# Attention scores per head on eight places of the TensorE array, with scores and transposed probabilities in four shared PSUM banks

## The chip, the cores and the metric

One Trainium2 chip, one core of it. The metric is the device time of one execution in microseconds; the kernel before took 2920.33 us as the median of three runs (2918.25 to 2920.56). TensorE is called PE here, VectorE DVE, ScalarE ACT, GpSimd POOL, and SyncE (which issues the transfers) SP.

## The reference

128 graphs of 64 nodes with 384 features, in float32, go through four layers, each followed by a residual and a layer norm:

```python
x = _layernorm(x + L0(x, adj))   # attention, 12 heads of 32; bias adj + adj
x = _layernorm(x + L1(x, adj))   # attention masked by adj > 0, bias beta * adj
x = _layernorm(x + L2(x, adj))   # directed graph convolution, two inner layers
x = _layernorm(x + L3(x, adj))   # attention like L0; bias adj
```

L0 and L3 compute, per graph and head, `softmax(q k^T * scale + bias) v`, then an output product with Wo and a bias bo; L1 has biases bq and bk, masks with `adj > 0` and has no output product. The weights are 384 x 384.

## The kernel before

The program runs five passes over all 8192 rows one after the other: an attention pass for L0, one for L1, two passes for L2, and an attention pass for L3. Only the attention passes (`attention_pass`, L143) are touched. Every pass reads its rows from memory and writes them back.

**Tiling.** A *unit* is 128 rows, that is two graphs; a *group* is four units (512 rows); a pass has 16 groups, 64 units. The first two and the last two groups are written out, the others run in a loop of pairs (`over_groups`, L49). The place of a unit within its group is called s, 0 to 3.

**The stages of a unit n on the engines.** Queries and keys are projected for a whole group (512 columns, L413) with the features on the partitions, values per unit (L407). Each projection is nine matmuls: three feature tiles and three products of high and low parts. ACT evicts the query (L555, L557) and the key. Of the key it makes two copies (L561, L564): one has the odd heads of each 64 features zeroed, the other the even ones, by the factor `even_odd`. The scores (L434) are twelve matmuls a unit: for each of three feature tiles, both graphs and both halves of 64 partitions, one product of 64 rows by 128 columns gives two heads. In the trace each shows as two records of 128 columns, 24 a unit. They go to `ps_s` (two banks). DVE scales them and adds the bias (L686), takes the maximum (L693) and in L0 and L3 the minimum (L695). POOL subtracts the maximum (L342), ACT takes the exponential (L607), DVE sums it (L700) and inverts the sum, POOL multiplies (L351, only in L0 and L3). PE transposes the probabilities, six transposes of 128 x 128 a unit (L447) into `ps_t` (two other banks), ACT evicts them (L602), and PE multiplies them with the values (L470 in L0 and L3, L466 in L1) into `ps_o`. In L0 and L3 ACT and DVE split the result into a high part (L617) and a low part (L733), PE multiplies with Wo (L485), and DVE adds the residual (L742), takes its statistics (L746, L749) and normalizes (L758). In L1 DVE scales the result (L729), POOL adds the residual (L331), and DVE takes the statistics.

**The order of the work is written out by hand.** Each engine executes its list in order and waits on semaphores. On PE a unit of the loop is:

```python
scores(n, par, s)
fill(i, par, s, 0)
probs_T(n - 1, ps % 2)
fill(i, par, s, 1)
values(n - 1, ppar, ps)
if wo: fill(i, par, s, 2)
scores_may(...)
if not wo: fill(i, par, s, 2)
output(n - 1, ps % 2)
```

`fill` issues the projections and the row transposes of the next groups. The table `BETWEEN` (L229) says which: between scores and transposes there is nothing at s=0 and s=1, and one projection at s=2 (a key) and s=3 (a value). On DVE a unit is: the residual and statistics of n-2, L686 and the maximum and minimum of n, the normalization of n-2, the low part of n-1, the sum of n, and the low parts of the next rows (`fill`). In L0 and L3 the residual of n-2 waits for the output product that PE issues at the end of its unit n-1.

**Waits around the change.** `probs_T` on PE (L439) waits for the probabilities (POOL, or ACT in L1) and for ACT to have evicted the halves of `ps_t`. `scores_may` (L417) waits until DVE has read the scores of the unit before.

**Start and passes.** `Shared` (L62) issues the four weights of L0 with one transfer each (`load`, L117) while DVE zeroes the value buffers (L115); the block ends when all engines are through. Each pass begins with its first rows (L250), two transfers of the value bias (L254), other small transfers, and the first edges (L263). The weights of the next pass are loaded during a pass, by the same `load`.

Of the kernel before, what the change touches and what calls it, by code (L numbers as in the profile page):

```python
# [21 lines left out]
P = 128  # L22
# [10 lines left out]
HEAD_STEP = 84  # L33
MASKED = -9000000000000000.0

SPLIT = ((0, 0), (1, 0), (0, 1))

# [24 lines left out]
class Shared:  # L62


    def __init__(self, nc, ctx, first_mats):
# [12 lines left out]
        self.even_odd = sb("even_odd", [P, 2])  # L78
# [6 lines left out]
        c_heads = nc.alloc_semaphore("c_heads")  # L85

        with nc.Block() as block:
# [5 lines left out]
            def _(pool):  # L93
# [8 lines left out]
                nc.gpsimd.memset(self.even_odd[:, :], 0.0).then_inc(c_heads, 1)  # L102
                pool.wait_ge(c_heads, 1)
                for head in range(4):
                    nc.gpsimd.memset(self.even_odd[32 * head:32 * head + 32, head % 2:head % 2 + 1], 1.0).then_inc(c_heads, 1)
# [37 lines left out]
def attention_pass(nc, tag, src, dst, adj, weights, scale, transposed, wo, bv, bo, beta, edge_factor, groups,  # L143
# [16 lines left out]
    with ExitStack() as ctx:  # L160
# [18 lines left out]
        k2 = [a.sb(f"k2{b}", [P, KT, 2, ROWS]) for b in range(2)]  # L179
        v2, even_odd = shared.v2, shared.even_odd  # L180
        qkb = a.sb("qkb", [P, 2, KT])
        kbm = a.sb("kbm", [P, 2, KT])
# [22 lines left out]
        c_zero = a.sem("c_zero")  # L205
        pe_w, act_w, dve_w = a.sem("pe_w"), a.sem("act_w"), a.sem("dve_w")
# [7 lines left out]
        dve_x, dve_off, dve_bias, dve_kb, dve_sc, dve_mx, dve_mn, dve_sum, dve_inv, dve_o = (  # L214
            a.sem(x) for x in ("dve_x", "dve_off", "dve_bias", "dve_kb", "dve_sc", "dve_mx", "dve_mn",
# [6 lines left out]
        n_small = 2 + (bo is not None) + (2 if row_bias_cols else 0) + (beta is not None)  # L222
# [140 lines left out]
        def _(pe):  # L363
# [1063 lines left out]
```

## Time and profile before

| what | value |
|---|---|
| median of three runs | 2920.33 us |
| the profiled execution | 2920.63 us |
| its span | 2918.9 us |
| mean granted PE clock | 0.963 of full |
| PE busy | 2676.6 us, 92% |
| DVE busy | 2204.6 us, 76% |
| POOL busy | 1906.2 us, 65% |
| ACT busy | 1441.8 us, 49% |

The span runs from the first to the last instruction of the profiled execution; the time of that execution also has what lies around it. The busy times are unions of an engine's instructions. The attention passes lie at about 9 to 655 us (L0), 661 to 1204 us (L1) and 2267 us to the end (L3); the two passes of L2 stand between. The loading of weights into the array (PEld) is shown apart from the matmuls (PE); both belong to one engine.

### The profile page before, as it was taken

How to read it: one execution, taken by the hardware profiler on the slowest of the kernel's cores; microseconds unless marked ns; L12 is line 12 of the kernel's file. 1: busy time of each engine (PE TensorE's matmuls, PEld its weight loads, DVE VectorE, ACT ScalarE, POOL GpSimd, SP SyncE). 2: the span in 40 equal slices, each digit the busy share in tenths (PEclk: the TensorE clock that was granted, in tenths of full speed). 3: DMA queues.
4: the chain of work that ended last, by engine and by line, in shares of the span. 5: the costliest groups of instructions: out<-in, count | busy, mean ns of one | idle time of the engine just before them, and what ended most of it. 6: DMA issues, size and time to landing. Idle time of an engine off the chain costs nothing. (4 is left out here: it accounts for less than half of the span.)

```text
span 2918.9 us, 67000 instructions
## 1 busy us (share of the span) xinstructions
PE 2676.6 (92%) x22942; PEld 2351.3 (81%) x22942; DVE 2204.6 (76%) x3795; ACT 1441.8 (49%) x2968; POOL 1906.2 (65%) x2229
## 2 busy tenths in 40 slices
PE   7999999977999999599999888888887899999996
PEld 6888888866778778599999877777776688888885
DVE  4888888874777777577777667777777488888886
ACT  4555555535566666344444344444444455555553
POOL 2766766762666666577777567767776267766766
PEclk9999999988999999699999989999999999999998
DMA  3222222113222222312212132222221122222211
GB/s 108 70 67 68 66 66 68 55 42 96 78 76 81 81 76 63 99 53 68 64 55 67 56 102 71 69 68 71 69 68 48 57 70 67 68 66 68 66 58 39
DMA packets 179134, 200.54 MB, mean 69 GB/s; under 512 B 56516, under 2 KB 179016, under 8 KB 179016
## 3 DMA queue, kind: packets, MB, share of 16 engines
q1 hardware_dynamic: 179016, 198.99, 22.2%
q8 instruction: 71, 1.16, 0.2%
q14 instruction: 47, 0.39, 0.0%
HBM read 136.03 MB, written 62.91 MB: 68 GB/s over the span
## 5 line engine op out<-in xcount | busy, mean ns | idle before, releaser
L413 PE MATMUL l_ps_p<-l_xT,l_w 128*128 128x512 f32 x2592 | 677.5, 406 | 6.5 <-DVE l_xT L655 4.5
L1088 PE MATMUL l_ps_h<-l_w,l_hT 128*128 128x384 f32 x3456 | 678.9, 342 | 0.0
L1088 PEld LDWEIGHTS l_ps_h<-l_w,l_hT 128*128 128x128 f32 x3456 | 612.6, 191 | 2.6
L413 PEld LDWEIGHTS l_ps_p<-l_xT,l_w 128*128 128x128 f32 x2592 | 467.8, 189 | 110.7 <-issue 8.3
L342 POOL TENSOR_TENSOR l_pr<-l_sc,l_st 128x768 f32<-128x768 f32 x192 | 289.4, 1507 | 368.7 <-DVE l_st L693 341.1
L1178 ACT ACTIVATE l_hp<-l_hf 128x384 fp32r<-128x384 f32 x256 | 134.7, 526 | 474.5 <-DVE l_hf L1300 470.4
L312 POOL TENSOR_TENSOR v<-v,l_bvs 128x768 f32<-128x768 f32 x192 | 368.6, 1920 | 0.0
L999 POOL TENSOR_TENSOR l_hp<-l_hf,l_hp 128x384 fp32r<-128x384 f32 x256 | 272.0, 1062 | 134.4 <-ACT l_hp L1178 131.7
L407 PE MATMUL l_ps_p<-l_w,l_xT 128*128 128x384 f32 x1728 | 349.5, 347 | 7.6 <-ACT l_k L561 3.7
L574 ACT ACTIVATE v<-l_ps_p 64x192 f32<-64x192 f32 x768 | 250.5, 326 | 188.0 <-PE l_ps_p L407 179.1
L407 PEld LDWEIGHTS l_ps_p<-l_w,l_xT 128*128 128x128 f32 x1728 | 291.6, 188 | 27.3 <-issue 8.8
L602 ACT ACTIVATE l_pT<-l_ps_t 128x512 f32<-128x512 f32 (+1 forms) x384 | 167.7, 491 | 182.9 <-PE l_ps_t L447 180.4
L485 PE MATMUL l_ps_y<-l_w,l_oT 128*128 128x384 f32 x1152 | 236.0, 351 | 23.8 <-DVE l_oT L733 20.5
L485 PEld LDWEIGHTS l_ps_y<-l_w,l_oT 128*128 128x128 f32 x1152 | 214.7, 196 | 30.0 <-issue 18.5
L351 POOL TENSOR_TENSOR l_pr<-l_pr,l_st 128x768 f32<-128x768 f32 x128 | 188.7, 1474 | 74.2 <-DVE l_st L711 68.1
L700 DVE TENSOR_REDUCE l_st<-l_pr 128x12 f32<-128x768 f32 x192 | 182.0, 948 | 37.8 <-ACT l_pr L607 37.7
L686 DVE SCALAR_TENSOR_TENSOR l_sc<-l_ps_s,l_sbias 128x768 f32<-128x768 f32 x192 | 183.9, 958 | 30.1 <-PE l_ps_s L434 24.1
L1300 DVE TENSOR_TENSOR l_hf<-l_ps_h,l_sides 128x384 f32<-128x384 f32 x256 | 142.3, 556 | 68.1 <-PE l_ps_h L1088 62.1
L564 ACT ACTIVATE l_k<-l_ps_p,even_odd 128x512 f32<-128x512 f32 x192 | 121.8, 685 | 138.1 <-PE l_ps_p L413 138.1
L693 DVE TENSOR_REDUCE l_st<-l_sc 128x12 f32<-128x768 f32 x192 | 183.0, 953 | 6.7
L607 ACT ACTIVATE l_pr<-l_pr 128x768 f32<-128x768 f32 x192 | 163.0, 849 | 44.5 <-POOL l_pr L342 42.3
L1104 PE MATMUL l_ps_c<-l_hp,l_aT 128*128 128x384 f32 x768 | 162.0, 345 | 23.7 <-POOL l_hp L999 22.9
(129 smaller groups left out, 4761.1 us busy)
## 6 DMA issues: line engine op xcount, KB each, us to landing
rows<-l_yo SPq DMA_DIRECT2D x256, 192.0 KB, 1.9
l_xa<-rows SPq DMA_DIRECT2D x64, 768.0 KB, 5.0
l_xr<-rows SPq DMA_DIRECT2D x192, 192.0 KB, 2.4
l_xa<-in_x SPq DMA_DIRECT2D x16, 768.0 KB, 4.8
l_xr<-in_x SPq DMA_DIRECT2D x64, 192.0 KB, 2.4
out<-l_yo SPq DMA_DIRECT2D x64, 192.0 KB, 1.9
l_edge<-in_adj SPq DMA_DIRECT2D x80, 128.0 KB, 2.3
raw<-in_L_gnn_Wq SPq DMA_DIRECT2D x3, 576.0 KB, 5.8
```

The costliest lines, as they stand in the source:

```text
L312: nc.gpsimd.tensor_tensor(got, got, bvs[:, :, :].unsqueeze(1).to_broadcast([P, GPU, PAIRS, 64]), ALU.add).then_inc(pool_v, 1)
L342: nc.gpsimd.tensor_tensor(pr[b][:, :, :], sc[b][:, :, :], st[b][:, 0, :].unsqueeze(2).to_broadcast([P, HEADS, NODES]), ALU.subtract).then_ ...
L351: nc.gpsimd.tensor_tensor(pr[b][:, :, :], pr[b][:, :, :], st[b][:, 5, :].unsqueeze(2).to_broadcast([P, HEADS, NODES]), ALU.mult).then_inc( ...
L407: last = nc.tensor.matmul(bank[:, :D], rows[:, l, t, o * P:(o + 1) * P], W[2][:, r, t, :], start=c + t == 0, stop=c == 2 and t == KT - 1)
L413: last = nc.tensor.matmul(bank[:, :], W[m][:, l, t, o * P:(o + 1) * P], rows[:, r, t, :], start=c + t == 0, stop=c == 2 and t == KT - 1)
L485: last = nc.tensor.matmul(ps_y[:, :D], oT[b][:, l, t, :], W[3][:, r, t, :], start=c + t == 0, stop=c == 2 and t == KT - 1)
L574: i = nc.scalar.activation(v2[gpar][64 * odd:64 * odd + 64, GPU * u + g2, :, 32 * odd:32 * odd + 32], got[:, :, odd, :], ACT.Copy)
L686: nc.vector.scalar_tensor_tensor(out=sc[b][:, :, :], in0=logits[:, :, :NODES], scalar=scale, in1=sbias[par][:, s, :].unsqueeze(1).to_broad ...
L693: nc.vector.tensor_reduce(st[b][:, 0, :], sc[b][:, :, :], AX.X, ALU.max).then_inc(dve_mx, 1)
L700: nc.vector.tensor_reduce(st[b][:, 2, :], pr[b][:, :, :], AX.X, ALU.add).then_inc(dve_sum, 1)
L999: nc.gpsimd.tensor_tensor(hp[b][:, m, 1, :], hf[b][:, m, :], hp[b][:, m, 0, :].bitcast(F32), ALU.subtract).then_inc(pool_h, 1)
L1088: last = nc.tensor.matmul(ps_h[m][:, :D], hT[gpar][:, l, t, s * P:(s + 1) * P], W[m][:, r, t, :], start=c + t == 0, stop=m != SELF and c = ...
```

## The change

Each head's scores become a matmul of their own: contraction over 32 partitions, 64 query columns loaded, 64 key columns moved. Four heads by two graphs stand on eight places of the array (`tile_position`), and the key needs one copy without zeroed heads. The heads are kept in the order of *slots*: slot 3m + t holds head 4t + m (`head_of` gives it), so that the four heads of a feature tile lie in four different banks. `ps_s` has four banks; each slot has 170 places, the first 64 for the scores, the next 64 for transposed probabilities, and `ps_t` is gone. The transposes become twelve a unit: per graph and pair of slots, 64 partitions by 128 columns. ACT evicts them per graph. Since scores and transposes share banks, PE waits before the transposes of n until DVE has read the scores of n + 1, and before the scores until ACT has evicted the transposes. The weights Wv and Wo, and the value bias, are loaded in the slots' order: by 12 transfers each (rows or columns by slot) in place of one or two. The factor `even_odd`, the two bias copies made with it, and their waits are gone.

```diff
-HEAD_STEP = 84
+HEAD_STEP = 170
+NATURAL, ROWS_BY_SLOT, COLUMNS_BY_SLOT = range(3)
+def head_of(slot):
+    return 4 * (slot % KT) + slot // KT
...
     def load(self, sp, mats, free=None):
-        for m, mat in enumerate(mats):
+        for m, (mat, order) in enumerate(mats):
             if free:
                 free(m)
-            sp.dma_start(self.raw[m][:, :, :], mat.rearrange("(t p) n -> p t n", p=P)).then_inc(self.s_raw[m], 16)
-            self.loads[m] += 1
+            if order == ROWS_BY_SLOT:
+                for slot in range(HEADS):
+                    t, b = divmod(slot, 4)
+                    head = head_of(slot)
+                    sp.dma_start(self.raw[m][32 * b:32 * b + 32, t, :], mat[32 * head:32 * head + 32, :]).then_inc(self.s_raw[m], 16)
+                self.loads[m] += HEADS
+            elif order == COLUMNS_BY_SLOT:
+                for t in range(KT):
+                    for q in range(4):
+                        natural = mat[t * P:(t + 1) * P, :].rearrange("p (k m d) -> p m k d", m=4, k=KT)[:, q, :, :]
+                        sp.dma_start(self.raw[m][:, t, 96 * q:96 * q + 96].rearrange("p (k d) -> p k d", k=KT),
+                                     natural).then_inc(self.s_raw[m], 16)
+                self.loads[m] += 4 * KT
+            else:
+                sp.dma_start(self.raw[m][:, :, :], mat.rearrange("(t p) n -> p t n", p=P)).then_inc(self.s_raw[m], 16)
+                self.loads[m] += 1
...
-        ps_s = a.ps("ps_s", [P, 2 * 512])
-        logits = ps_s[:, 8:8 + HEADS * HEAD_STEP].rearrange("p (h x) -> p h x", x=HEAD_STEP)
-        ps_t = a.ps("ps_t", [P, 2 * 512])
+        ps_s = a.ps("ps_s", [P, 4 * 512])
+        by_head = ps_s[:, 8:8 + HEADS * HEAD_STEP].rearrange("p (h x) -> p h x", x=HEAD_STEP)
+        logits, turned = by_head[:, :, :NODES], by_head[:, :, NODES:2 * NODES]
...
-            for odd in range(2):
-                heads = bv.rearrange("(a h o d) -> a h o d", a=1, o=2, d=32)[:, :, odd, :]
-                sp.dma_start(bvs[64 * odd:64 * odd + 64, :, 32 * odd:32 * odd + 32],
-                             heads.to_broadcast([64, PAIRS, 32])).then_inc(s_small, 16)
+            for slot in range(HEADS):
+                h, odd = divmod(slot, 2)
+                head = bv.rearrange("(a d) -> a d", a=1)[:, 32 * head_of(slot):32 * head_of(slot) + 32]
+                sp.dma_start(bvs[64 * odd:64 * odd + 64, h, 32 * odd:32 * odd + 32],
+                             head.to_broadcast([64, 32])).then_inc(s_small, 16)
...
                 if counted(n):
                     pe.wait_ge(dve_sc, n)
+                if counted(2 * (n - 1)):
+                    pe.wait_ge(act_pT, 2 * (n - 1))
...
             def scores(n, par, s):
                 for t in range(KT):
                     for g in range(GPU):
-                        for r in range(2):
-                            c, q = s * P + g * NODES, slice(64 * r, 64 * r + 64)
-                            h = PAIRS * r + 2 * t
-                            last = nc.tensor.matmul(logits[g * NODES:(g + 1) * NODES, h:h + 2, :NODES],
-                                                    qT[par][q, t, c:c + NODES], k2[par][q, t, :, c:c + NODES],
-                                                    start=True, stop=True)
+                        for m in range(4):
+                            c, q = s * P + g * NODES, slice(32 * m, 32 * m + 32)
+                            last = nc.tensor.matmul(logits[g * NODES:(g + 1) * NODES, KT * m + t, :],
+                                                    qT[par][q, t, c:c + NODES], kT[par][q, t, c:c + NODES],
+                                                    start=True, stop=True, tile_position=(32 * m, g * NODES))
...
                 pe.wait_ge(pool_p if wo else act_e, n + 1)
+                pe.wait_ge(dve_sc, n + (2 if inside(n + 1, units) else 1))
+                pe.sem_inc(pe_waited, 1)
                 for h in range(PAIRS):
-                    if h in (0, 4):
-                        if counted(2 * n - 1 + (h == 4)):
-                            pe.wait_ge(act_pT, 2 * n - 1 + (h == 4))
-                    last = nc.tensor.transpose(ps_t[:, h * P:(h + 1) * P], pr[b][:, 2 * h:2 * h + 2, :], ident[:, :])
-                    if h in (3, 5):
-                        last.then_inc(pe_t, 1)
+                    for g in range(GPU):
+                        q = slice(g * NODES, (g + 1) * NODES)
+                        last = nc.tensor.transpose(turned[:, PAIRS * g + h, :], pr[b][q, 2 * h:2 * h + 2, :], ident[q, q])
+                        if h == PAIRS - 1:
+                            last.then_inc(pe_t, 1)
...
-                        for j in range(2):
-                            if row_bias_cols:
-                                i = nc.scalar.activation(k2[gpar][:, o, j, :], bank[:, :], ACT.Identity,
-                                                         bias=kbm[:, j, o:o + 1], scale=even_odd[:, j:j + 1])
-                            else:
-                                i = nc.scalar.activation(k2[gpar][:, o, j, :], bank[:, :], ACT.Copy,
-                                                         scale=even_odd[:, j:j + 1])
+                        if row_bias_cols:
+                            i = nc.scalar.activation(kT[gpar][:, o, :], bank[:, :], ACT.Identity, bias=qkb[:, 1, o:o + 1])
+                        else:
+                            i = nc.scalar.activation(kT[gpar][:, o, :], bank[:, :], ACT.Copy)
...
-                for half, (lo, hi) in enumerate(((0, 4), (4, 6))):
-                    act.wait_ge(pe_t, 2 * n + half + 1)
+                for g in range(GPU):
+                    act.wait_ge(pe_t, 2 * n + g + 1)
...
-                    nc.scalar.activation(pT[b][:, lo:hi, :], ps_t[:, lo * P:hi * P].rearrange("p (h q) -> p h q", q=P),
+                    nc.scalar.activation(pT[b][:, :, g * NODES:(g + 1) * NODES], turned[:, PAIRS * g:PAIRS * (g + 1), :],
```

Wq and Wk are loaded in one transfer as before; Wv of L0 and L3 by rows, Wv of L1 and Wo of L0 and L3 by columns. The passes of L2 are not changed.

## Rows read from the trace of the kernel before

**Rows 1.** The page's part 1: engine, busy us (share of the span) xinstructions.

```profile
PE 2676.6 (92%) x22942; PEld 2351.3 (81%) x22942; DVE 2204.6 (76%) x3795; ACT 1441.8 (49%) x2968; POOL 1906.2 (65%) x2229
```

**Rows 2.** Busy time by stretch, layer 3: window, length, busy (count) per engine, PEclk, DMA share.

```profile
2303.00:2867.00 564.00, 559.55 (x5259) 472.56 (x5251) 479.09 (x768) 306.12 (x658) 392.23 (x355) 1.00 0.21 62
```

**Rows 3.** Groups by line and form, PE: busy us, mean ns | idle before, releasers.

```profile
L434 PE MATMUL l_ps_s<-l_k,l_qT 64*64 64x128 f32 x4608 | 174.3, 282 | 0.8 <-DVE l_sc L686 0.8
...
L447 PE MATMUL l_ps_t<-ident,l_pr 128*128 128x128 f32 x1152 | 166.2, 281 | 12.8 <-ACT l_pr L607 9.5 <-POOL l_pr L351 3.2
...
L470 PE MATMUL l_ps_o<-l_pT,v 128*64 128x64 f32 x3072 | 123.7, 228 | 11.1 <-ACT l_pT L602 9.2
```

**Rows 4.** Timeline of layer 3, a unit at s=0: start us, us, engine, line.

```profile
2527.95 0.64 PEld L434 LDWEIGHTS l_ps_s<-l_k,l_qT 64*64 64x64 f32 x24 [0.24 <-issue]
...
2528.05 0.56 DVE L742 TENSOR_TENSOR l_res<-l_ps_y,l_xr 128x384 f32<-128x384 f32 x1 [0.92 <-PE l_ps_y L485]
...
2528.83 0.64 PEld L447 LDWEIGHTS l_ps_t<-ident,l_pr 128*128 128x128 f32 x6 [0.24 <-issue]
...
2529.58 0.96 DVE L686 SCALAR_TENSOR_TENSOR l_sc<-l_ps_s,l_sbias 128x768 f32<-128x768 f32 x1
```

**Rows 5.** Timeline of layer 3, units at s=2 and s=3.

```profile
2509.64 0.96 DVE L686 SCALAR_TENSOR_TENSOR l_sc<-l_ps_s,l_sbias 128x768 f32<-128x768 f32 x1
...
2510.86 0.81 PEld L447 LDWEIGHTS l_ps_t<-ident,l_pr 128*128 128x128 f32 x6
...
2519.53 1.53 PEld L407 LDWEIGHTS l_ps_p<-l_w,l_xT 128*128 128x128 f32 x9 [0.17 <-issue]
...
2520.29 0.96 DVE L686 SCALAR_TENSOR_TENSOR l_sc<-l_ps_s,l_sbias 128x768 f32<-128x768 f32 x1
...
2521.05 0.75 PEld L447 LDWEIGHTS l_ps_t<-ident,l_pr 128*128 128x128 f32 x6
...
2523.71 0.83 PEld L470 LDWEIGHTS l_ps_o<-l_pT,v 128*64 128x64 f32 x24 [0.42 <-ACT l_pT L602]
...
2526.27 1.75 PE L485 MATMUL l_ps_y<-l_w,l_oT 128*128 128x384 f32 x9
```

**Rows 6.** Timeline of layer 1, units at s=0 and s=1.

```profile
917.58 0.64 PEld L447 LDWEIGHTS l_ps_t<-ident,l_pr 128*128 128x128 f32 x6 [0.17 <-issue]
...
917.73 0.96 DVE L686 SCALAR_TENSOR_TENSOR l_sc<-l_ps_s,l_sbias 128x768 f32<-128x768 f32 x1
...
924.84 0.64 PEld L447 LDWEIGHTS l_ps_t<-ident,l_pr 128*128 128x128 f32 x6 [0.17 <-issue]
...
925.08 0.96 DVE L686 SCALAR_TENSOR_TENSOR l_sc<-l_ps_s,l_sbias 128x768 f32<-128x768 f32 x1
```

**Rows 7.** Timeline of layer 0, its last group.

```profile
624.84 0.55 DVE L733 TENSOR_TENSOR l_oT<-l_ps_o,l_oT 128x384 fp32r<-128x384 f32 x1
...
625.53 2.87 PE L485 MATMUL l_ps_y<-l_w,l_oT 128*128 128x384 f32 x9 [1.42 <-DVE l_oT L733]
```

**Rows 8.** Busy time by stretch, line L434 alone: window, length, PE (count), PEld (count).

```profile
2527.94:2528.00 0.06, 0.05 (x4) 0.05 (x4) 1.00 1.00 282
```

**Rows 9.** Timeline of the start, layer 0.

```profile
2.38 0.49 SPq L122 DMA_DIRECT2D raw<-in_L_gnn_Wo  x1
...
5.78 2.62 DVE L115 MEMSET v<- 128x3072 f32 x1 [0.59 <-issue]
...
9.23 1.39 SPq L254 DMA_DIRECT2D l_bvs<-in_L_gnn_bv  x2
```

**Rows 10.** Busy time by stretch, end of layer 0 and layer 2; PEclk behind POOL.

```profile
614.00:632.00 18.00, 12.88 (x127) 10.77 (x126) 15.00 (x26) 4.42 (x8) 13.24 (x13) 0.72 0.15 46
...
1715.00:1722.00 7.00, 4.94 (x31) 4.62 (x30) 6.49 (x17) 1.66 (x3) 3.77 (x10) 1.00 0.17 50
```

**Rows 11.** Timeline, PE alone, end of layer 0 and layer 2.

```profile
616.43 3.22 PE L485 MATMUL l_ps_y<-l_w,l_oT 128*128 128x384 f32 x9 [2.42 <-DVE l_oT L733]
...
1719.02 0.66 PE L1073 MATMUL l_ps_a<-ident,l_wide 128*128 128x128 f32 x4 [2.06 <-DVE l_wide L1280]
```

More of the change, by code:

```diff
@@ L101, in _ @@
                                         base=0, pattern=[[-1, P]], channel_multiplier=1).then_inc(c_const, 1)
[L102 to L105, printed above, removed]
             @block.vector
@@ L178, in attention_pass @@
         qT = [a.sb(f"qT{b}", [P, KT, ROWS]) for b in range(2)]
-        k2 = [a.sb(f"k2{b}", [P, KT, 2, ROWS]) for b in range(2)]
-        v2, even_odd = shared.v2, shared.even_odd
+        kT = [a.sb(f"kT{b}", [P, KT, ROWS]) for b in range(2)]
+        v2 = shared.v2
         qkb = a.sb("qkb", [P, 2, KT])
-        kbm = a.sb("kbm", [P, 2, KT])
         sc = [a.sb(f"sc{b}", [P, HEADS, NODES]) for b in range(2)]
@@ L205, in attention_pass @@
         c_zero = a.sem("c_zero")
+        pe_waited = a.sem("pe_waited")
         pe_w, act_w, dve_w = a.sem("pe_w"), a.sem("act_w"), a.sem("dve_w")
@@ L213, in attention_pass @@
             a.sem(x) for x in ("act_x", "act_qk", "act_v", "act_e", "act_pT", "act_o"))
-        dve_x, dve_off, dve_bias, dve_kb, dve_sc, dve_mx, dve_mn, dve_sum, dve_inv, dve_o = (
-            a.sem(x) for x in ("dve_x", "dve_off", "dve_bias", "dve_kb", "dve_sc", "dve_mx", "dve_mn",
+        dve_x, dve_off, dve_bias, dve_sc, dve_mx, dve_mn, dve_sum, dve_inv, dve_o = (
+            a.sem(x) for x in ("dve_x", "dve_off", "dve_bias", "dve_sc", "dve_mx", "dve_mn",
                                "dve_sum", "dve_inv", "dve_o"))
@@ L220, in attention_pass @@
             a.sem(x) for x in ("pool_sub", "pool_p", "pool_ve", "pool_rs", "pool_v", "pool_xr", "pool_res"))
-        n_small = 2 + (bo is not None) + (2 if row_bias_cols else 0) + (beta is not None)
+        n_small = HEADS + (bo is not None) + (2 if row_bias_cols else 0) + (beta is not None)
         steps = NM * KT
@@ L471, in values @@
                                                     v2[par][:, GPU * s + g, 2 * t + r, :],
-                                                    pT[s % 2][:, KT * r + t, g * NODES:(g + 1) * NODES],
+                                                    pT[s % 2][:, 2 * t + r, g * NODES:(g + 1) * NODES],
                                                     start=True, stop=True)
@@ L538, in _ @@
                 act.wait_ge(s_small, 16 * n_small)
-                act.wait_ge(dve_kb, 2)
             def rows_T(g, gpar, t, bank):
@@ L686, in softmax_max @@
                 nc.vector.scalar_tensor_tensor(
-                    out=sc[b][:, :, :], in0=logits[:, :, :NODES], scalar=scale,
+                    out=sc[b][:, :, :], in0=logits, scalar=scale,
                     in1=sbias[par][:, s, :].unsqueeze(1).to_broadcast([P, HEADS, NODES]), op0=ALU.mult, op1=ALU.add,
@@ L726, in low_part @@
                         dve.wait_ge(pool_res, n - 1)
-                    heads = scaled[b][:, :].rearrange("p (h d) -> p h d", h=HEADS)
-                    rinv = st[b][:, 5, :].unsqueeze(2).to_broadcast([P, HEADS, D // HEADS])
-                    nc.vector.tensor_tensor(heads, ps_o[:, :D].rearrange("p (h d) -> p h d", h=HEADS), rinv,
+                    heads = scaled[b][:, :].rearrange("p (k m d) -> p m k d", m=4, k=KT)
+                    rinv = st[b][:, 5, :].rearrange("p (m k) -> p m k", k=KT).unsqueeze(3).to_broadcast([P, 4, KT, D // HEADS])
+                    nc.vector.tensor_tensor(heads, ps_o[:, :D].rearrange("p (m k d) -> p m k d", m=4, k=KT), rinv,
                                             ALU.mult).then_inc(dve_o, 1)
@@ L759, in normed @@
                                         ALU.mult).then_inc(dve_y, 1)
-            if row_bias_cols or beta is not None:
+            if beta is not None:
                 dve.wait_ge(s_small, 16 * n_small)
-            if row_bias_cols:
-                for j in range(2):
-                    nc.vector.tensor_scalar(kbm[:, j, :], qkb[:, 1, :], even_odd[:, j:j + 1], 0.0, ALU.mult, ALU.add).then_inc(dve_kb, 1)
             for t in range(KT):
@@ L1385, in graph_layers @@
     l0, l1, l2, l3 = (lambda k, layer=layer: ins[f"L{layer}_gnn_{k}"] for layer in range(4))
-    w0 = [l0(k) for k in ("Wq", "Wk", "Wv", "Wo")]
-    w1 = [l1(k) for k in ("Wq", "Wk", "Wv")]
-    w2 = [[l2(m)[k] for m in ("Wl", "Wr", "Ws")] for k in range(2)]
-    w3 = [l3(k) for k in ("Wq", "Wk", "Wv", "Wo")]
+    slots = (NATURAL, NATURAL, ROWS_BY_SLOT, COLUMNS_BY_SLOT)
+    w0 = list(zip((l0(k) for k in ("Wq", "Wk", "Wv", "Wo")), slots))
+    w1 = list(zip((l1(k) for k in ("Wq", "Wk", "Wv")), (NATURAL, NATURAL, COLUMNS_BY_SLOT)))
+    w2 = [[(l2(m)[k], NATURAL) for m in ("Wl", "Wr", "Ws")] for k in range(2)]
+    w3 = list(zip((l3(k) for k in ("Wq", "Wk", "Wv", "Wo")), slots))
     ctx = ExitStack()
```

7 lines of the change are left out of this document (2 added, 5 removed).

## Prediction

> **What bounds the kernel now.** The page's engine lines come first: TensorE (PE) is busy 92% of the span [rows 1]. A share over the whole span mixes five passes, so the stage table is next: inside the last pass (layer 3), away from its ends, PE is busy 559.55 of 564 us at the full granted clock [rows 2]. In the attention passes nearly every microsecond added to PE is therefore added to the end, and a microsecond taken from another engine is worth nothing. The groups by line then say what the touched operations cost PE [rows 3]: the scores (L434) 174.3 us for 192 units, 0.91 us a unit; the transposes (L447) 166.2 us, 0.87; the values (L470) 123.7 us for 128 units, 0.97. Before the first two PE hardly waits (0.8 and 12.8 us in all).
>
> Last come the timelines of single units, to see what stands between the scores of unit n and the transposes of unit n-1. At place s=0 of a group [rows 4] nothing does: weight loads for the scores begin at 2527.95, those for the transposes at 2528.83. VectorE meanwhile does the residual of unit n-2 (L742, from 2528.05, released by the output product that PE has just finished), then its statistics, and only at 2529.58 the pass over the scores (L686), which ends at 2530.54. Today nobody on PE waits for that end before the next unit's scores.
>
> **The change, part by part.**
>
> *The new wait.* Scores and transposed probabilities now share four banks, so the transposes of n-1 wait until VectorE has read the scores of n. In layers 0 and 3 at s=0 that end lies 2530.54 - 2528.83 = 1.71 us behind the point where PE is ready [rows 4]. A release from VectorE to PE takes about 0.1 us (L733 ends at 625.39, the first product of L485, which waited for it, starts behind its load at 625.53 [rows 7]). So 1.8 us. Making the scores shorter gains nothing here: L686 stands behind the residual, and the residual behind PE's output product. The order is rigid: output, residual, statistics, scores read, transposes. Queued behind the waiting transposes on PE are one projection, the values, more projections and the output; ScalarE's evictions and, through the output, VectorE's next residual wait for those, so the whole loop moves by the stall. s=1 is the same: it too has no projection between scores and transposes. One of the two has 15 such units a pass and the other 14 (the first unit has no predecessor, the second waits for POOL anyway): 58 units in two passes x 1.8 = 104 us. In a pass's last group places 2 and 3 have no projection either, but PE waits for other things there too: four units at 1.2 of the 1.8, 5 us. Together **+109**.
>
> At s=2 and s=3 a projection lies between. There the scores' read ends 0.26 us before the transposes' loads (2510.60 against 2510.86) and 0.20 us behind them (2521.25 against 2521.05) [rows 5]. At s=3 the values wait 0.42 us for ScalarE's eviction today, which takes up that 0.3; shorter scores start the projection 0.3 us earlier, and a mode switch (below) takes part of it. I take -0.2 a unit x 60 = **-12**; bounds -0.35 and +0.35.
>
> *Layer 1* has no output product; VectorE's chain hangs on the values of the unit before. The distance is 917.73 + 0.96 - 917.58 = 1.11 us at s=0 and 925.08 + 0.96 - 924.84 = 1.20 at s=1 [rows 6]; with the release 1.2 and 1.3. 30 units: +38. Places 2 and 3: -0.2 x 30 = -6. One key eviction instead of two frees a bank sooner, where PE waits little: -3. Together **+29**.
>
> *Scores.* 24 records of 128 columns on four places become 48 of 64 columns on eight. Today's 0.91 us less the 0.28 of one record leaves 0.63 for 24, 27 ns apart. The nearest row with 64 columns is the values: (0.97 - 0.23)/23 = 32 ns on two places, 64 ns a place [rows 3]. Six records on each of eight places: 0.38 + 0.23 = 0.61 us, 0.3 less than now. If places did not overlap further, 48 x 27 to 32 ns would make 1.3 to 1.5 us; a gain beyond half is excluded by the columns, which stay. I take 0.3, the row nearest in shape. Only s=2 and s=3 can use it, and it is in the -0.2 above.
> The Trainium skill's page "TensorE: Matmul & The Clock Gate", section "Wait — 56ns, not 53.3ns?", says that matmuls never start less than about 25 ns apart, however small; by it, as an estimate, the 48 would take at least 1.2 us and the sum would come out near the third rival's. The trace does not agree: four matmuls of the scores fall into 0.06 us [rows 8].
>
> *Transposes.* Six of 128x128 become twelve of 64 rows, 64 moving columns, on two places. Now 0.64 us of loads [rows 4]; at the values' 32 ns, 12 x 32 = 0.38. But the array now changes its form on the way back to the projection too. Such changes show as 0.24 us of idle before the scores' loads [rows 4] and 0.17 before the projection behind them [rows 5]; the second is the same change, so I take it. Net -0.26 + 0.17 = -0.09 x 192 = **-17**; bounds -0.26 (no cost of the form) and +0.81 (each half transposition as long as a whole one, 12 x 0.107, and the form).
>
> *VectorE and ScalarE.* The scores' read and the evictions move as many elements as before; the second key eviction goes (it counted above). Nothing else of it is on the path.
>
> *Loads.* The start has 26 weight transfers instead of 4. The last issue now ends at 2.87 us and took 0.49; a bias transfer takes 1.39/2 = 0.70; the start's block ends on VectorE's memset at 8.40 us [rows 9]. 22 more issues at 0.49 to 0.70 end at 13.7 to 18.3 us, 5 to 10 later than that memset; smaller pieces may issue faster, down to nothing lost. I take +6, by the row of the weights, which are nearest. The twelve small bias pieces ahead of the edge load can hold up the other two passes by as much as they add to SyncE's queue, a few microseconds, or not at all: +1. **+7** in all. Weights for later passes load beside running work and cost nothing; without that cover they would cost the same few microseconds.
>
> *The clock.* PE's new idle stretch in layers 0 and 3 is about 1.8 us and the 0.3 that the scores got shorter: 2.1 us, in a loop that now has none. Rows on both sides [rows 10, 11]: around an idle stretch of 2.06 us the granted clock stayed 1.00; in the drain of layer 0, with one of 2.42 us and other waits beside it, it averages 0.72, in part the lower level, 1.2 GHz, and nine output products behind that wait took 3.22 us, against 1.75 at the full clock [rows 5]. So one fall costs about 1.5 us. The new stretch is nearest to the row of 2.06, but it comes 58 times. I take a third of them, 20 x 1.5 = **+30**; bounds 0 and 58 x 1.5 = 87.
>
> **Sum:** 109 - 12 + 29 - 17 + 7 + 30 = 146 us. The profiled execution took 2920.63 us (span 2918.9, 1.7 around it), 0.3 over the median of 2920.33. 2920.6 + 146 = **3067 us**, 5% slower.
>
> **The rivals.**
> 1. *The clock falls after most stalls.* Place: the projections behind the wait at s=0 and s=1. For it: 2.1 us is close to the 2.42 that went with a fall. Against: the row of 2.06. Price: 87 in place of 30, 3124, and some falls lasting longer: up to **3140**.
> 2. *Faster: the wait is free.* If VectorE had read the scores by the time that PE is ready, only the gains stay: 0.3 + 0.26 us on 192 units, 108 us, less the changes of form (0.17 x 192 = 33) and the start (7), so 68: **2853**. It decides once L686 ends within 68 / 88 = 0.8 us of PE being ready instead of 1.7 (58 + 30 stalls), that is if it ran before the residual. Against: it is written behind the residual, and the residual waits for PE itself [rows 4].
> 3. *The scores on eight places don't overlap* (the change doesn't do what it says): 1.3 to 1.5 us a unit. At s=0 and s=1 that hides in the wait and even shortens the idle stretch; at places 2 and 3, 90 units, it costs 0.5 and the lost 0.2: +63, less half of the clock's 30: about **3115**. For it: the mean spacing today is 27 ns. Against: [rows 8].
>
> **How the numbers follow.** The forecast 0.66, the clock rival 0.14, no overlap 0.13, faster 0.04, an unforeseen cover that leaves no change 0.03. The forecast's own bounds: no fall of the clock (-30), a free start (-7) and -0.35 instead of -0.2 at the other places (90 units, -14) make 3016; half of the stalls followed by a fall (+14) and transposes that gain nothing (+50) make 3131. The range takes in the third rival and the first: 3005 to 3140. 0.2% is 6 us, about what a measurement of this kernel can tell from no change: faster 0.04, within 0.03, slower 0.93.
>
> **What would show it.** Right: PE's idle before the transposes named as VectorE's L686, some 1.8 us at two of four places in layers 0 and 3 and 1.2 in layer 1, nothing at the others; scores' union about 0.6 us a unit; a group of four units of layer 3 lasting some 3 to 4 us longer; the granted clock of that pass a little under 1.0. Wrong: the transposes released by POOL or by nobody; scores over 1 us; a clock near 0.9 (first rival); layers 0 and 3 as long as before.

## The result and the profile after

The kernel after takes 3158.43 us (median of 4 runs, 3153.11 to 3173.26), beside 2920.19 for the kernel before on the same chip: a ratio of 1.0824, 95% interval 1.0802 to 1.0847, so 238 us more. The forecast was 3067 (3005 to 3140): the sign was right, the time lies 18 us outside the range. The profiled execution took 3161.56 us, 3 over the median.

The page of after, part 1 (engines) and two lines of part 3 (DMA queues: packets, MB, share):

```profile
PE 2707.4 (86%) x28702; PEld 2363.3 (75%) x28702; DVE 2172.6 (69%) x3793; ACT 1345.5 (43%) x2824; POOL 1906.5 (60%) x2224
...
q1 hardware_dynamic: 193048, 199.00, 20.7%
q8 instruction: 233, 3.82, 0.5%
```

Against [rows 1] TensorE is busy 31 us more in a span 241 us longer: most of what came is idle time. The queue of instruction transfers (code that is brought to the engines) has 233 transfers here; in the page of before its line is:

```profile
q8 instruction: 71, 1.16, 0.2%
```

The groups of PE by line (busy us, mean ns | idle before, releasers):

```profile
L431 PE MATMUL l_ps_p<-l_xT,l_w 128*128 128x512 f32 x2592 | 721.3, 426 | 6.4 <-DVE l_xT L671 4.5 <-ACT l_qT L576 1.0 <-ACT l_qT L574 0.7
...
L453 PE MATMUL l_ps_s<-l_kT,l_qT 32*64 32x64 f32 x9216 | 154.0, 236 | 62.8 <-issue 62.8
...
L467 PE MATMUL l_ps_s<-ident,l_pr 64*128 64x64 f32 x2304 | 120.8, 239 | 165.8 <-DVE l_sc L702 94.9 <-issue 65.1 <-POOL l_pr L369 3.2
```

Scores (now L453) and transposes (now L467) are shorter than in [rows 3]: 0.80 us a unit against 0.91, 0.63 against 0.87. Two idle times are new. The one before the transposes, 165.8 us against 12.8, is the wait that the prediction saw coming. The one before the scores, 62.8 us against 0.8, has no releaser, and the prediction has no place for it.

Both stand in this timeline of PE in layer 3 of after (start us, us, engine, line, idle before):

```profile
2620.64 1.75 PE L505 MATMUL l_ps_y<-l_w,l_oT 128*128 128x384 f32 x9
2625.27 0.77 PE L453 MATMUL l_ps_s<-l_kT,l_qT 32*64 32x64 f32 x48 [2.88 <-issue]
2627.34 0.34 PE L467 MATMUL l_ps_s<-ident,l_pr 64*128 64x64 f32 x4 [1.30 <-DVE l_sc L702]
2628.53 0.69 PE L467 MATMUL l_ps_s<-ident,l_pr 64*128 64x64 f32 x8 [0.84 <-issue]
2629.15 4.21 PE L431 MATMUL l_ps_p<-l_xT,l_w 128*128 128x512 f32 x9
...
2638.95 0.78 PE L453 MATMUL l_ps_s<-l_kT,l_qT 32*64 32x64 f32 x48
2641.62 0.59 PE L467 MATMUL l_ps_s<-ident,l_pr 64*128 64x64 f32 x12 [1.89 <-DVE l_sc L702]
2642.14 2.37 PE L431 MATMUL l_ps_p<-l_xT,l_w 128*128 128x512 f32 x9
...
2649.59 0.78 PE L453 MATMUL l_ps_s<-l_kT,l_qT 32*64 32x64 f32 x48
2650.30 2.37 PE L431 MATMUL l_ps_p<-l_xT,l_w 128*128 128x512 f32 x9
2652.60 0.59 PE L467 MATMUL l_ps_s<-ident,l_pr 64*128 64x64 f32 x12
2653.12 2.37 PE L431 MATMUL l_ps_p<-l_xT,l_w 128*128 128x512 f32 x9
...
2660.06 0.78 PE L453 MATMUL l_ps_s<-l_kT,l_qT 32*64 32x64 f32 x48
```

At 2638.95 (s=1) PE waits 1.89 us for VectorE's pass over the scores, as forecast. At 2649.59 (s=2) a projection covers it. But at 2625.27, the head of the next pass through the loop of two groups, PE stands still for 2.88 us with no releaser named, its transposes come in two pieces with another such stretch between, and the nine projections behind take 4.21 us instead of 2.37. The granted clock in those nine projections is 0.50, the lower of its two levels (1.2 GHz of 2.4). Such a head comes 15 times, five in each of the three attention passes (six passes through the loop, so five jumps back).

The transfers fall inside the loop. In one pass of layer 3 of after (2625.20 to 2716.00 us) the list of DMA queues has ten of them:

```profile
q8 instruction: 10, 0.16, 0.8%
```

In a pass of layer 3 of before (2492.00 to 2567.50 us) the data queue's line is followed by the issues; there is no instruction queue:

```profile
q1 hardware_dynamic: 4393, 4.95, 21.6%
issues: line engine op xcount, KB each, median us to landing
```

### The profile page after: what moved, and what is told of

Its sections match the earlier page's. It is cut to its first block and busy times, and to the rows that moved or that the text cites. A ratio compares the mean times of both kernels' runs of the same rounds, so it can differ in the third digit from the quotient of the medians.

```text
span 3159.8 us, 78573 instructions
## 1 busy us (share of the span) xinstructions
PE 2707.4 (86%) x28702; PEld 2363.3 (75%) x28702; DVE 2172.6 (69%) x3793; ACT 1345.5 (43%) x2824; POOL 1906.5 (60%) x2224
## 3 DMA queue, kind: packets, MB, share of 16 engines
q8 instruction: 233, 3.82, 0.5%
## 5 line engine op out<-in xcount | busy, mean ns | idle before, releaser
L431 PE MATMUL l_ps_p<-l_xT,l_w 128*128 128x512 f32 x2592 | 721.3, 426 | 6.4 <-DVE l_xT L671 4.5
L431 PEld LDWEIGHTS l_ps_p<-l_xT,l_w 128*128 128x128 f32 x2592 | 495.6, 200 | 123.9 <-ACT l_xT L562 5.3
L618 ACT ACTIVATE l_pT<-l_ps_s 128x384 f32<-128x384 f32 x384 | 167.6, 489 | 400.4 <-PE l_ps_s L467 399.3
L467 PE MATMUL l_ps_s<-ident,l_pr 64*128 64x64 f32 x2304 | 120.8, 239 | 165.8 <-DVE l_sc L702 94.9
L467 PEld LDWEIGHTS l_ps_s<-ident,l_pr 64*128 64x128 f32 x2304 | 96.2, 146 | 208.1 <-issue 208.1
L505 PE MATMUL l_ps_y<-l_w,l_oT 128*128 128x384 f32 x1152 | 237.9, 353 | 13.7 <-DVE l_oT L748 10.3
L505 PEld LDWEIGHTS l_ps_y<-l_w,l_oT 128*128 128x128 f32 x1152 | 216.1, 199 | 20.5 <-issue 12.2
L453 PEld LDWEIGHTS l_ps_s<-l_kT,l_qT 32*64 32x64 f32 x9216 | 126.7, 135 | 116.9 <-issue 116.6
L453 PE MATMUL l_ps_s<-l_kT,l_qT 32*64 32x64 f32 x9216 | 154.0, 236 | 62.8 <-issue 62.8
L748 DVE TENSOR_TENSOR l_oT<-l_ps_o,l_oT 128x384 fp32r<-128x384 f32 x128 | 71.4, 558 | 198.2 <-ACT l_oT L633 195.6
```

Source lines behind the costliest of these rows:

```text
L431: last = nc.tensor.matmul(bank[:, :], W[m][:, l, t, o * P:(o + 1) * P], rows[:, r, t, :], start=c + t == 0, stop=c == 2 and t == KT - 1)
L453: last = nc.tensor.matmul(logits[g * NODES:(g + 1) * NODES, KT * m + t, :], qT[par][q, t, c:c + NODES], kT[par][q, t, c:c + NODES], start= ...
L467: last = nc.tensor.transpose(turned[:, PAIRS * g + h, :], pr[b][q, 2 * h:2 * h + 2, :], ident[q, q])
L505: last = nc.tensor.matmul(ps_y[:, :D], oT[b][:, l, t, :], W[3][:, r, t, :], start=c + t == 0, stop=c == 2 and t == KT - 1)
```

## The experiments

All times are medians beside runs of the kernel before on the same chip (2920 us each time).

**1 to 4: the two suspects, one at a time.** First, after with TensorE's loop written out:

```
-            over_groups(pe, groups, group)
+            for i in range(groups):
+                group(i, i // 2, i % 2)
```

> The changed kernel with the attention passes' TensorE program written out for all 16 groups in place of the loop over pairs; nothing else differs. Theory (the longer loop body is fetched anew in every pass through the loop, and TensorE waits for it at the loop's head): the idle time before the first scores of a pair that is put down to issue (62.8 us before L453 in all) and most of the 65.1 us of issue before the transposes go, some falls of the clock with them: 3060 to 3100 us. Rival (those idle stretches belong to the new wait or to waits on a register's value that merely are named issue): the stretches stay in the same places, 3140 us or more.

3055.87 us, ratio 1.0465 (1.0448 to 1.0482): 102.6 us less than after, just below the range of the text. The stretches at the heads are gone (groups of PE by line of this kernel):

```profile
L431 PE MATMUL l_ps_p<-l_xT,l_w 128*128 128x512 f32 x2592 | 696.3, 414 | 6.5 <-DVE l_xT L672 4.5 <-ACT l_qT L577 1.0 <-ACT l_qT L575 0.7
...
L453 PE MATMUL l_ps_s<-l_kT,l_qT 32*64 32x64 f32 x9216 | 151.1, 234 | 0.0
...
L467 PE MATMUL l_ps_s<-ident,l_pr 64*128 64x64 f32 x2304 | 115.4, 233 | 168.2 <-issue 101.7 <-DVE l_sc L703 61.3 <-POOL l_pr L369 3.2
```

The idle time before the scores accounts for 63 us, the slower projections behind it for 25 (721.3 - 696.3), slower scores and transposes for 8. The idle time before the transposes stays: 168 us, though the profile now names VectorE for a part of it only. This kernel has 199 instruction transfers, fewer than after has, though its program is longer: in after the code of the loop comes again in each pass.

The control, the same edit made to the kernel before:

> The kernel before with the same writing out of TensorE's loop. Theory: its loop body is not fetched again in any pass through the loop (71 instruction transfers in all), so writing it out gains nothing: 2915 to 2930 us, with more instruction transfers. Rival (writing out speeds up TensorE for another reason, so that the first experiment does not tell of fetching): 2900 us or less.

2916.61 us, 0.9987 (0.9978 to 0.9997). Writing out saves some 3.5 us by itself, and brings 154 instruction transfers in place of 71; the other 99 us are something that after has and before has not.

Next, the kernel before with the wait alone, so with its own banks, four places and whole transposes:

```
                 pe.wait_ge(pool_p if wo else act_e, n + 1)
+                pe.wait_ge(dve_sc, n + (2 if inside(n + 1, units) else 1))
```

> The kernel before with one line added: TensorE waits, before the transposes of a unit, until VectorE has read the scores of the next. Scores, transposes, loads and banks stay as before. Theory (this wait is the larger part of the loss): transposes at s=0 and s=1 start 2.6 us behind the scores' start in layers 0 and 3 and about 2 us in layer 1, no issue stretches at the head of the loop, 3050 to 3090 us. Rival (the code that is fetched again and the new shapes are the larger part): under 3000 us.

3081.42 us, 1.0555 (1.0537 to 1.0573): 161 us. Groups of PE by line of this kernel, whose transposes are L448:

```profile
L448 PE MATMUL l_ps_t<-ident,l_pr 128*128 128x128 f32 x1152 | 167.7, 283 | 165.4 <-DVE l_sc L687 120.7 <-issue 35.6 <-POOL l_pr L351 6.2
```

165.4 - 12.8 [rows 3] = 153 us of new idle time. The other 8 fit the granted clock, which in this kernel's table of stretches stands at 0.98 in layer 3 (first to last scores), where in the kernel before it is 0.99:

```profile
2403.20:3056.80 653.60, 588.22 (x5449) 492.41 (x5448) 485.92 (x804) 311.40 (x670) 412.02 (x373) 0.98 0.18 56
```

The instruction queue has 71 transfers, as before. So the wait and the heads together, 161 + 103, are more than the 238 that the change cost. If the two add up, its useful parts give back about 26 us (22 by the two kernels written out, 161 against 139); that is a difference of runs, not measured by itself.

Then after with a projection moved into the empty gap between scores and transposes, taken from the gap behind:

```
-BETWEEN = (((), (0,), (1, 2)), ((), (3,), (4, 5)), ...
+BETWEEN = (((0,), (1, 2), ()), ((3,), (4, 5), ()), ...
```

> The changed kernel with one projection put between scores and transposes at s=0 and s=1 too (the table BETWEEN: the first chunk of these places takes the projection that stood behind the transposes). Theory: the wait is covered there in layers 0 and 3 and in layer 1 (1.9 us of projection against 1.8 and 1.2), the fetch at the loop's head stays: 3010 to 3060 us, with idle before the transposes released by VectorE near 10 us. Rival (the wait is only moved: the values then wait for ScalarE's eviction or the output for VectorE): 3120 us or more.

A miss, and the rival's number: 3167.49 us, 1.0858 (1.0840 to 1.0876). Groups of PE by line, with L505 the output product:

```profile
L431 PE MATMUL l_ps_p<-l_xT,l_w 128*128 128x512 f32 x2592 | 724.7, 427 | 64.1 <-DVE l_xT L671 60.5 <-ACT l_qT L576 1.9 <-ACT l_qT L574 0.9
...
L505 PE MATMUL l_ps_y<-l_w,l_oT 128*128 128x384 f32 x1152 | 242.8, 357 | 87.2 <-DVE l_oT L748 83.8 <-DVE l_res L757 3.4
...
L467 PE MATMUL l_ps_s<-ident,l_pr 64*128 64x64 f32 x2304 | 121.6, 243 | 26.5 <-issue 17.2 <-DVE l_sc L702 7.0 <-ACT l_pr L623 0.2
```

The wait before the transposes went (165.8 to 26.5 us), but the output product, now right behind the values, waits for their low part, and in layer 1 the projections wait for a row transpose's low part. Cover that is taken from another gap opens that gap.

**5 to 7: what the wait consists of.** In these three TensorE's loop is written out, so 3055.87 us is the base. First one piece in every gap of s=0 and s=1:

```
+BETWEEN = (((0,), (1,), (2,)), ((3,), (4,), (5,)), ((6,), (7,), (8, 9)), ...
```

> The kernel after with TensorE's attention loop written out (3055.9 us by an earlier run) and the work for the next group spread one piece to a gap in the first two units of a group: a q projection of 2.37 us between scores and transposes, a row transpose of 0.65 us between transposes and values, a projection between values and output. Theory (the wait for DVE's reading of the scores is idle TensorE time that a projection can fill): the 1.85 us of the first two units goes, 0.4 to 0.5 us comes in its place at the values, which wait for ACT's 0.9 us eviction with only a row transpose as cover; over the 64 such units of L0 and L3 about -85 us, so 2970 us, L1 between -15 and +15. Rival (the chain through DVE bounds the unit, and any cover only moves the idle time to another wait, as the earlier reordering did): the same idle time shows at the projections and the values, 3040 to 3070 us.

2962.14 us, 1.0145 (1.0127 to 1.0163): -94 us. Groups of PE by line:

```profile
L490 PE MATMUL l_ps_o<-l_pT,v 128*64 128x64 f32 x3072 | 128.7, 233 | 34.4 <-ACT l_pT L619 34.4
L467 PE MATMUL l_ps_s<-ident,l_pr 64*128 64x64 f32 x2304 | 115.5, 234 | 26.1 <-issue 16.1 <-DVE l_sc L703 7.6 <-ACT l_pr L624 0.2
```

The wait was idle time that a projection can fill, and what comes in its place is smaller: 34.4 us before the values, where only a row transpose is left to cover ScalarE's eviction.

The other way to shorten it is VectorE's order, reading the scores ahead of the residual of two units ago:

```
-                    residual(n - 2, count, s % 2)
-                    softmax_max(n, par, s)
+                    take_scores(n, par, s)
+                    residual(n - 2, count, s % 2)
+                    softmax_max(n, s)
```

> The kernel after with the loop written out (3055.9 us) and one order changed on DVE: it reads the scores of a unit before it adds the residual of two units earlier, not behind it. Theory (the wait is scores 0.78 us, then DVE's residual and its statistics that stand before the reading, then the reading of 0.96 us): transposes start 1.85 to 1.95 us after the scores' start in the first two units of L0 and L3 instead of 2.53 to 2.64, so about -0.7 us on 64 units, -45 us, 3010 us; L1 as it is (no residual work of that place stands before its reading). Rival (DVE has no slack, so what is put behind the reading makes the next unit's probabilities or output late by as much): 3045 to 3070 us, with new idle time at the output or at the transposes waiting for POOL's probabilities.

3010.98 us, 1.0316 (1.0298 to 1.0335): -45 us, as the theory said. A unit at s=1 in its timeline of PE, layer 3:

```profile
2569.03 0.78 PE L453 MATMUL l_ps_s<-l_kT,l_qT 32*64 32x64 f32 x48
2570.91 0.59 PE L467 MATMUL l_ps_s<-ident,l_pr 64*128 64x64 f32 x12 [1.10 <-DVE l_sc L703]
```

1.88 us from scores to transposes instead of 2.67. So 0.8 us of the wait was the residual and its statistics, and the rest, 1.10 us of it idle, is the scores and their reading.

> Both of the edits before together: one piece of the next group's work to a gap, and the scores read before the residual. If the wait is what a projection covers, the second edit adds little to the first, since a projection of 2.37 us already covers 1.9 us: within 15 us of the first one's time. If DVE's chain bounds the unit, the two add up to no more than the better of them. Faster than the kernel before (2920 us) on neither theory.

Both together: 2967.76 us, 1.0167 (1.0149 to 1.0185), 6 us behind the first edit alone. Once a projection covers the reading, the order on VectorE has nothing left to give.

**8 to 10: is it the length of the loop?** The kernel before, with two tiny matmuls ahead of each score matmul, whose places the scores overwrite:

```
+                            for again in range(2):
+                                nc.tensor.matmul(logits[g * NODES:(g + 1) * NODES, h, :8], ...
```

> The kernel before, with nothing of the change but the length of TensorE's loop: ahead of each of the 12 score matmuls of a unit stand two tiny ones (8 columns, into places that the scores overwrite). A pass through the loop has then 1910 matmul records in L0 and L3 and 1744 in L1, against 1526 and 1360. Their own time, 48 records of 13 to 27 ns a unit with nothing that hides them, is 0.6 to 1.3 us on 192 units, so +120 to +250 us, part of it hidden where the transposes wait anyway. Theory (a loop body too long is fetched again in every pass through it): the instruction queue shows more than the 71 transfers of before, about 150 to 230, and every second group of L0 and L3 begins with an idle stretch of 2.5 to 4.5 us without a releaser before the scores' line; L1, at 1744, may go either way and tells where the limit lies. Rival (the stretches of the kernel after come from something else in it, such as the form of the array): 71 to 75 transfers and no such stretch.

> The kernel before with the 24 tiny matmuls ahead of each unit's scores and its loop written out, beside the same pad in the loop (3174.1 us). Theory (the loop's repeated fetch): the stretches at the score line (80 us) go, and 80 to 100 us of the time with them: 3075 to 3095 us, so the pad's own work costs some 160 to 175 us of the 254. Rival (the stretches come with the pad's instructions however they are reached): 3165 to 3180 us.

> The kernel before with half that pad, one tiny matmul ahead of each score matmul: 1718 matmul records in a pass through the loop of L0 and L3, 1552 in L1. Theory (a limit between 1526 records, which stay, and 1744, which are fetched again): L1 at 1552 is either not fetched again, or only in part; L0 and L3 at 1718 near the kernel with 1744 in L1, each of 6 passes with 2 or 3 more transfers. So 71 transfers if the limit is above 1718, some 110 if it lies between, 120 or more if below 1552. Time: half of the pad's own 160 to 175 us, so 3000 to 3010 us without any fetch, 3035 to 3075 us with it in L0 and L3 alone. Rival (the fetch grows in proportion to the length, with no limit): transfers midway between 71 and 263 and idle stretches half as long at every second group.

The counts in these texts take everything on TensorE together (1526 is 708 matmuls, 708 loads and 110 others, on semaphores and registers), and they are too low for the pads: a pad matmul leaves two matmul and two load records, not one of each. By the table of stretches, a pass through the loop of layers 0 and 3 has, in matmul records (the loads are as many), 708 before, 900 with one tiny matmul, 948 in after and 1092 with two; of layer 1, 72 fewer each (636, 828, 876, 1020). Two of these stretches, a pass of layer 3 in after and one of layer 1 with one tiny matmul (edges can take in a record of the neighbour):

```profile
2625.20:2716.00 90.80, 79.98 (x948) 66.25 (x948) 63.29 (x104) 37.17 (x82) 52.64 (x48) 0.92 0.19 57
```

```profile
955.50:1030.50 75.00, 67.58 (x829) 55.27 (x828) 47.82 (x75) 38.82 (x80) 40.90 (x41) 0.95 0.22 68
```

Two tiny ones in the loop: 3174.09 us, 1.0871 (1.0852 to 1.0890), 263 transfers, more of both than the text expected. The same written out: 3054.82, 1.0462 (1.0445 to 1.0480), below the range of its text. So the loop costs 119 us by itself in a kernel that has nothing of the change but the length. One tiny matmul in the loop: 3103.91, 1.0632 (1.0614 to 1.0650), 224 transfers, above both ranges of its text, as all three layers are fetched again and not two. This kernel was not written out. By an estimate, half of the written-out pad's 138 us (3054.82 - 2916.61) on top of 2916.61 would make 2986, so the loop costs 118 us here: as much as with twice the pad. The lines of the instruction queue in the pages of these three, in that order:

```profile
q8 instruction: 263, 4.31, 0.6%
```

```profile
q8 instruction: 226, 3.70, 0.5%
```

```profile
q8 instruction: 224, 3.67, 0.5%
```

And a loop head of the last kernel, layer 3 (L494 the output product, L435 the tiny matmuls, L443 the scores):

```profile
2574.85 1.75 PE L494 MATMUL l_ps_y<-l_w,l_oT 128*128 128x384 f32 x9
2580.36 0.61 PE L435 MATMUL l_ps_s<-l_k,l_qT 64*64 64x8 f32 x16 [3.77 <-issue]
2583.56 0.40 PE L435 MATMUL l_ps_s<-l_k,l_qT 64*64 64x8 f32 x8 [2.58 <-issue]
2583.79 1.54 PE L443 MATMUL l_ps_s<-l_k,l_qT 64*64 64x128 f32 x24
```

The rival, a cost in proportion to the length, falls. All three layers have such a stretch at each jump back, layer 1 with 828 records too, where the stretch of 75.00 us above has nine transfers:

```profile
q8 instruction: 9, 0.15, 0.8%
```

So the limit lies between 708 and 828; where in between was not tried. Transfers alone don't stop PE: the written-out pad makes 226 of them without such a stretch.

**11 and 12: what is left of the change.** The kernel of experiment 5, with the values of layers 0 and 3 taken in two halves, each behind its own eviction:

```
-                pe.wait_ge(act_pT, 2 * (n + 1))
+                pe.wait_ge(act_pT, 2 * n + 1 if wo else 2 * (n + 1))
...
+                    if wo and j == KT * 2:
+                        pe.wait_ge(act_pT, 2 * (n + 1))
```

> The kernel with one piece to a gap and the loop written out (2962.1 us), and in L0 and L3 the values taken by halves of the probabilities: the 12 matmuls of the first half wait only for ACT's first eviction, those of the second for the second. That kernel's plain groups of L3 last 38.4 us against 37.8 before, with 34.4 us idle before the values' line. Theory (this wait is what is left in the loop, while eight places and half-height transposes save 0.21 us a unit): the idle time of that line falls from 34.4 to under 10 us, groups of L3 37.6 to 37.8 us, 2935 to 2945 us in all, so still slower than before by the later start of L0 and L1. Rival (the eight places give nothing once their change of form is paid): groups stay at 38.2 or more, 2955 to 2965 us.

2929.48 us, 1.0033 (1.0022 to 1.0043). The time lies below the range of the text. The idle time before the values falls to 9.2 us, and a group of layer 3 lasts 37.42 us, against 37.84 before, where every other one has 37.7 (first scores of two groups, this kernel, then the kernel before):

```profile
2557.00 0.78 PE L453 MATMUL l_ps_s<-l_kT,l_qT 32*64 32x64 f32 x48
...
2594.42 0.78 PE L453 MATMUL l_ps_s<-l_kT,l_qT 32*64 32x64 f32 x48
```

```profile
2527.95 0.89 PE L434 MATMUL l_ps_s<-l_k,l_qT 64*64 64x128 f32 x24
...
2565.79 0.45 PE L434 MATMUL l_ps_s<-l_k,l_qT 64*64 64x128 f32 x8
```

So the shorter scores and transposes do pay here, by up to 0.1 us a unit, once little waits for the shared banks; what eight places alone give of it was not tried. Layer 1 still loses (its groups last 31.9 to 32.0 us against 31.4 to 31.5), and the start is later. For layer 1 the row transposes were put behind the values:

```
+        if not wo:
+            AHEAD = (("q", 0), ("q", 1), ("x", 0), ("q", 2), ("k", 0), ("x", 1), ...
```

> The kernel with values by halves (2929.5 us), and in L1 the row transposes put behind the values instead of between transposes and values, so that a projection of 1.83 to 2.37 us stands in each of the two gaps that wait (for DVE's reading, and for ACT's eviction). That kernel's groups of L0 and L3 last 37.4 us against 37.8 before, those of L1 32.0 against 31.45, with 20.4 us idle before the values of L1. Theory (that idle time is what L1 still loses): it falls to under 5 us, groups of L1 at 31.0 to 31.5 us, 2913 to 2921 us in all: level with the kernel before (2920) or a few us faster, and level with the kernel before written out (2916.6). Rival (in L1 DVE's low part of the rows comes so late behind the softmax that the projection behind it waits, as in the first reordering): groups of L1 at 32 or more, 2928 to 2945 us.

A miss, and the rival's number: 2940.83 us, 1.0072 (1.0059 to 1.0086); groups of layer 1 last 32.72 us. Its timeline of layer 1, a unit at s=1, shows why:

```profile
875.25 0.78 PE L456 MATMUL l_ps_s<-l_kT,l_qT 32*64 32x64 f32 x48
...
876.51 0.67 DVE L680 TENSOR_TENSOR l_xT<-l_ps_p,l_xT 128x512 fp32r<-128x512 f32 x1
877.10 0.55 DVE L770 BATCH_NORM_STATS2 l_ln<-l_res 128x6 f32<-128x384 f32 x1
...
877.95 0.96 DVE L711 SCALAR_TENSOR_TENSOR l_sc<-l_ps_s,l_sbias 128x768 f32<-128x768 f32 x1
...
879.01 0.59 PE L470 MATMUL l_ps_s<-ident,l_pr 64*128 64x64 f32 x12 [0.68 <-issue]
```

The values now end later, so VectorE's work on them, the row transpose's low part and the statistics all stand ahead of the scores' reading (L711, to 878.91), and the transposes wait for it once more. The profile puts that wait to nobody; the row of VectorE tells. No version of the change tried here beats the kernel before; that one written out, at 2916.61, is the fastest of all, by 0.1%.

## Why the prediction was wrong

**The step that failed** is the change of the scores from 24 records to 48 and of the transposes from 6 to 12. The prediction costed them as time on the array (0.61 us, -0.09 us) and never as instructions in a loop: the sum had no term for the code, and no rival had it. It adds 240 matmul records, with as many loads, to a pass through the loop of two groups. With 708 in a pass no code is transferred in it; with 828 or more it is fetched again in each pass (9 to 11 transfers), and PE stands at the head. That is 102.6 us, or 6.8 for each of 15 jumps. The Trainium skill's page "Runtime: NRT & Kernel Launch", section "Instruction fetch mechanics", says that TensorE holds 2048 instructions, refilled in blocks of 16 KiB, and that a taken branch to a target outside the window must fetch before it goes on. The trace agrees on the stall and on the size of a transfer (3.82 MB in 233, 16 KB each). It does not agree on 2048 as the limit for a loop: the 828 matmuls, 828 loads and 88 other instructions of layer 1's padded loop make 1744, and they were fetched again.

Without that the sum holds. Forecast: +146. Measured, written out against written out: 3055.87 - 2916.61 = **+139**. The closeness is in part luck, as two terms missed in opposite directions: the clock was put too dear, and the gains at s=2 and s=3 of layers 0 and 3 too large.

- *The wait*, +109 and +38 in layer 1: the wait alone brought 153 us of idle time against 147. At s=1 of after the transposes start 2.67 us behind the scores, and their loads 0.11 behind the end of VectorE's read. Right, in the place and in the size; the two rows:

```profile
2640.52 0.96 DVE L702 SCALAR_TENSOR_TENSOR l_sc<-l_ps_s,l_sbias 128x768 f32<-128x768 f32 x1
...
2641.59 0.48 PEld L467 LDWEIGHTS l_ps_s<-ident,l_pr 64*128 64x128 f32 x12 [2.00 <-issue]
```

- *The clock*, +30: too high. The table of stretches gives layers 0, 1 and 3 a mean granted clock of 0.99 before, 0.98, 0.99 and 0.98 with the wait alone. One hundredth of that mean is two hundredths of the stretch at the lower of its two levels, half of which is lost at most: 6.5 us in each of layers 0 and 3, some 13 in all with means so rounded. In after the means are 0.94, 0.95 and 0.94, but most of that belongs to the loop's heads: written out, they are 0.98, 0.99 and 0.97, some 20 us at most by the same reckoning. The first rival, which reaches 3140, is wrong about the cause though nearest to the time.
- *Places s=2 and s=3*, -0.2 a unit, with the transposes' -0.09 beside it: too much. In layers 0 and 3 s=2 gains 0.18 for both (10.47 us from scores to scores in after, 2649.59 to 2660.06; the kernel before 10.65) and s=3 some 0.1 at most (9.2 against 9.2 to 9.3). In layer 1 s=2 gains 0.5 (8.8 against 9.3) and s=3 0.1.
- *Scores*, 0.61 us a unit: mis-sized, 0.80 measured. The next projection starts 0.71 us behind their start, 0.82 before, so 0.11 is won and not 0.3. The third rival, no overlap, falls with it: 48 records in 0.78 us.
- *Transposes*, -0.09: start to the next projection 0.52 us, against 0.57 (s=2) to 0.62 (s=0, s=1) before: right, or a little less.
- *Loads*, +6 at the start: right. The issues of the weights end at 15.45 us, PE's first instruction starts at 16.14 us instead of 8.72, and its first scores at 52.38 instead of 45.72, so +6.7.

The second rival (the wait is free) falls: PE waited. The order on VectorE sets the length of the wait, as the prediction said, but reading the scores ahead of the residual does not free it, as the prediction took for granted: 0.8 us a unit went and 1.10 us of idle time stayed.

## What to carry to other kernels

Count the instructions that a change adds to a loop on an engine, not only their time: when a pass through TensorE's loop grew from 708 matmul records to 828 or more, each jump back cost 7 to 8 us, and the price came at once, not by degrees. Transfers of the instruction queue inside the loop, together with idle time without a releaser at the loop's first line, are its marks; writing the loop out was the test here, and the cure. Two users of one bank add a wait whose length is set by the order on the engine that reads; move work into the gap from where nothing else needs cover, or the wait only changes its place.

## What was not expected of the hardware

- The loop's limit: no transfer in a pass with 708 matmul records, nine with 828, eleven with 1092, and the cost hardly differs between the two padded loops (118 us, an estimate, and 119).
- The clock falls behind such a head: the nine projections behind idle stretches of 2.88, 1.30 and 0.84 us took 4.21 us at a granted clock of 0.50; behind a single one of 1.89 us they took 2.37 at 1.00.
- 48 matmul records of 32 rows on eight places take 0.78 us, 24 of 64 rows on four 0.89: twice the places gave an eighth.
- A wait for VectorE is put to "issue" in many units (101.7 of 168.2 us in the written-out kernel); only VectorE's row beside it, ending some 0.1 us earlier, shows what was waited for.
